# Expert tiles: GpSimd's two result scatters without the wait for TensorE's step signal

## The reference

```python
x = x + attention(layernorm(x), w_lhs, w_rhs)       # softmax((x*w_lhs)(x*w_rhs)^T) x
h = layernorm(x)
logits = h @ router_w.T                              # 4096 x 8, softmax, top 2, gates normalised
hid = gelu_tanh(h @ w_fc[e] + b_fc[e])               # 128 -> 512
y = hid @ w_proj[e] + b_proj[e]                      # 512 -> 128
x = x + sum over the row's two experts of gate * y
```

## Time and profile before

| | us |
|---|---|
| median of 3 runs | 387.25 (387.25 to 387.86) |
| the profiled execution | 387.9 |
| its span, first to last instruction | 386.0 |
| mean granted TensorE clock | 0.914 of full |
| attention | about 0 to 196 |
| expert tiles | about 196 to 366 |
| loading, adding and storing the results | about 366 to 386 |

### The profile page before, as it was taken

How to read it: one execution, slowest core, us unless ns; L and a number is a source line. 1 busy time by engine, 2 the same in 40 slices (tenths; PEclk the granted TensorE clock), 3 DMA queues, 4 the chain that set the end, 5 groups by cost and what they waited for, 6 DMA issues and landing times.

```text
span 386.0 us, 8026 instructions
## 1 busy us (share of the span) xinstructions
PE 312.9 (81%) x2292; PEld 276.0 (72%) x2293; DVE 206.9 (54%) x794; ACT 198.9 (52%) x405; POOL 186.4 (48%) x242
## 2 busy tenths in 40 slices
PE   2689899998799999998778396799999999996000
PEld 1468788876697879886667374699999999996000
DVE  4657488696566677778466433733332333332045
ACT  4216438796037653354538422777776777772000
POOL 7200044092835635376728566555555555557300
PEclk9989998999799998998969798999999999999555
DMA  7910000003100001010321132132222222111099
GB/s 219 440 50 2 1 3 0 3 0 110 36 21 30 28 16 34 23 43 21 94 75 51 41 101 88 56 99 84 78 85 81 77 76 77 42 43 48 28 313 339
DMA packets 17157, 29.48 MB, mean 76 GB/s; under 512 B 3808, under 2 KB 13024, under 8 KB 16864
## 3 DMA queue, kind: packets, MB, share of 16 engines
q1 hardware_dynamic: 12224, 18.46, 14.7%
q0 software_dynamic: 4896, 10.58, 8.3%
HBM read 16.36 MB, written 12.66 MB: 75 GB/s over the span
## 4 chain that ended last, share of the span: by engine, by line
PE 63%; DVE 10%; ACT 7%; another core or an unknown queue 7%; issue 5%; DMA 5%; SPq 1%; DVEq 0%; POOL 0%; ACTq 0%; POOLq 0%
PE av_ps L1211 16%; PE av_ps L1019 14%; PE sc_ps L1194 4%; PE sc_ps L1196 4%; PE sc_ps L1195 4%; PE bank L998 3%; DMA raw_proj<-results 3%; PE bank L999 3%; PE bank L1000 3%; ACT prob L877 2%; PE bank L1182 2%; PE sc_ps L998 2%; PE bank L1011 2%; PE sc_ps L999 2%
## 5 line engine op out<-in xcount | busy, mean ns | idle before, releaser
L835 POOL DMA_INDIRECT results<-prob,result_row x80 | 76.6, 957 | 58.4 <-PE sc_ps L1196 33.0
L749 POOL DMA_INDIRECT slots<-stage,slot x64 | 62.7, 980 | 50.7 <-ACT prob L877 26.7
L1211 PE MATMUL av_ps<-raw_proj,raw_fc 128*128 x640 | 80.3, 280 | 5.3 <-issue 4.3
L1211 PEld LDWEIGHTS av_ps<-raw_proj,raw_fc 128*128 128x128 f32 x640 | 76.5, 196 | 7.4 <-issue 6.8
L955 ACT ACTIVATE raw_fc<-sc_ps,bfc,scale_down 128x256 f32<-128x256 f32 x160 | 77.2, 571 | 2.1 <-PE sc_ps L1196 2.1
L1019 PEld LDWEIGHTS av_ps<-h_all,prob 128*128 128x128 f32 x512 | 70.5, 199 | 8.8 <-issue 4.3
L1019 PE MATMUL av_ps<-h_all,prob 128*128 128x137 f32 x512 | 73.4, 291 | 3.8 <-issue 3.8
L1602 DVE TENSOR_TENSOR h_all<-av_ps,bpr 128x256 f32<-128x256 f32 x40 | 17.0, 425 | 89.7 <-PE sc_ps L1196 60.8
L947 ACT ACTIVATE h_all<-bank 128x512 f16<-128x512 f16 x40 | 23.8, 598 | 58.3 <-PE sc_ps L1196 27.9
L1194 PE MATMUL sc_ps<-h_all,wfc_hi 128*128 128x256 f16 x160 | 44.8, 280 | 3.3 <-issue 2.1
L1195 PE MATMUL sc_ps<-h_all,wfc_hi 128*128 128x256 f16 x160 | 44.7, 280 | 2.7 <-issue 2.7
(11 more groups left out here) (176 smaller groups left out, 528.0 us busy)
## 6 DMA issues: line engine op xcount, KB each, us to landing
slots_in<-slots SPq DMA_DIRECT2D x40, 130.0 KB
raw_fc<-in_w_fc_dram SPq DMA_DIRECT2D x1, 2048.0 KB, 11.0
raw_proj<-in_w_proj_dram SPq DMA_DIRECT2D x1, 2048.0 KB, 15.1
raw_fc<-results SPq DMA_DIRECT2D x2, 1024.0 KB, 6.9
raw_proj<-results SPq DMA_DIRECT2D x2, 1024.0 KB, 11.2
out_dram<-res SPq DMA_DIRECT2D x4, 512.0 KB, 5.0
res<-in_x_dram SPq DMA_DIRECT2D x3, 512.0 KB, 5.5
results<-prob,result_row POOLq DMA_INDIRECT x80
```

What stands on the lines that cost most here:

```text
L749: pool.indirect_dma_start(out=slots[:, :], out_offset=bass.IndirectOffsetOnAxis(ap=slot[:, n, k:k + 1], axis=0), in_=stage[:, b % 2, t, k, ...
L835: pool.indirect_dma_start(out=results[:, :], out_offset=bass.IndirectOffsetOnAxis(ap=result_row[a][:, h:h + 1], axis=0), in_=gated[a][h], ...
L1211: mm = pe.matmul(o, hid[:, a % NH, c, s], wpr[:, e, c, :], start=(c == 0 and h == 0), stop=(c == HC - 1), skip_group_check=True)
```

## The change

The wait on `stepped` goes. GpSimd's step k now waits only for `row_made` and `gated_made` of tile k-4, inside `give_back`.

```diff
                 for i in LAST_SCATTERS.get(k, ()):
                     dispatch(B - 1, i)
                 if k >= 4:
-
-                    if tile_there(k):
-                        pool.wait_ge(stepped, up_at(k))
                     give_back(k - 4, (k - 4) % NR)
```

## The result

The changed kernel takes 404.74 us (median of 4 runs, 403.59 to 406.33) against 387.56 us for the kernel before, measured with it: ratio 1.0433, 95% interval 1.0378 to 1.0488. It is slower by 17 us, where 2 us less were forecast and 390.2 was the top of the range.

The account below looks back on a forecast made before the run. Expert stage taken as TensorE-bound in its plain part, elsewhere held by long runs of GpSimd's indirect DMAs. Terms 0 + 0 - 2.1 + 0.1 = -2.0 us took the profiled 387.9 to 385.9, as median 385.3 us; range 382.9 to 390.2.

Parts of the forecast that it names:

- Step 1: All 36 waits removed (k = 4 to 39): the issue saved is hidden behind TensorE's tile of 3.32 us, 0.
- Step 2: Expert stage's TensorE-bound stretch: two scatters per tile merely start later in the period; 0, bounds -1 to +3 us.
- Step 3: Last tiles: a run of six scatters replaces eight, so the last signal comes sooner; 2.1 us gained, bounds 0.9 and 4.4.
- Step 4: Start of the expert stage: dispatches and scatters fuse into longer runs, only rests move; +0.1 us taken from three pricings.
- the first two: Early part's pricings: by mean progress of TensorE, a gain of 1.8 us; if rests count as before, 0.
- The third, by runs: Early part's pricing with two issues free per run and 1.2 us for each beyond: 2.4 or 4.8 us slower.
- Rival B: Early part: fused runs cost 2.4 to 4.8 us, less 2.1 at the tail; 387.6 to 390, at worst 392; chance 0.32.
- Rival C: TensorE's late signals have their own cause and GpSimd merely waits in step; nothing changes, 387.2 us; chance 0.15.

Follow-up runs that it names:

- the fours: Kernel before, wait kept, but in steps 8 to 35 GpSimd waits every other step, then sends two tiles' four scatters: 399.51 us, ratio 1.0313 on a holding chip.
- the paced tail: Kernel before plus one wait: in step 41 GpSimd awaits TensorE's very last down step before sending tile 37's rows: 385.58 us, ratio 0.9935 on a holding chip.

## Why the prediction was wrong

- **What bounds the kernel now.** Right in its main reading, that long runs of indirect DMAs hold TensorE or its signals; the fours and the paced tail showed it by moving GpSimd's issues and nothing else. Wrong in its last words, "runs of two do not": they hold as well, for 1.4 to 1.5 us an issue, and the kernel before keeps clear of it by only 0.1 to 0.2 us. Its own trace has such signals, at 248.75 and 251.99.
- **Step 1, the wait itself, 0.** Not measured apart; where nothing is held, the whole change gives a ratio of 0.9972 (0.9941 to 1.0003), so the 36 waits are worth at most some 2 us of issuing.
- **Step 2, the plain part. This is the step that failed**: "the same two per tile, the same rest, another phase ... Price 0", with 3 us as the upper bound. It measured 15.2 us when changed alone and 14.3 in the whole. The phase was the price. I forecast the start of a pair well (2 us behind the signal) and saw that the next signal then falls into it, but took one punctual signal, 1.5 us into a run, as proof. That is just where the first issue's 1.43 us is over. The rows had the other evidence: dividing 7.2 and 11.4 us by 5 and 8 gives 1.44 and 1.43.
- What I missed behind it is the feedback. A held signal makes two gates come together, two gates make a run of four, and a run of four holds the next signal. My bound of 0.1 us a tile presupposed that disturbances die out.
- **Step 3, the tail, -2.1.** The size came out (-2.3 in the whole), the way did not: there is no run of six, still one of eight (from 367.21). The last signal came inside it, 8.5 us (six times 1.43) behind its first issue, where it came 11.4 us behind before; why it waited for fewer issues is open, so the size came out by luck. Alone, the edit gains nothing; its first step sends four in a row, which hold a signal by 2.7 us.
- **Step 4, the early part, +0.1 between -1.8 and +4.8.** Measured +3.8 in the trace (4.2 from the first up step's signal on) and 4.3 alone. The bounds held, the value was wrong, and it did not lie "between the first two" prices, which are -1.8 and 0. The third, by runs (2.4 or 4.8 us, the latter for {15,10}), had the right shape: the trace has fifteen issues and then ten.
- **The sum** -2.0 was measured as +17.2. **Rival B**, slower by fused runs, was the right kind and sign (chance 0.31 for slower), but it put the fused runs into the early part alone, gave the plain part 3 us at most for signals held "a little", and stopped at 392 (its own terms add up to 393).
- **Rival C and the skill.** The rows show signals held behind GpSimd's runs on two chips or more, and none held on three others. The Trainium skill, "SBUF — State Buffer", section "SBUF: two separate sides", has TensorE wait for nobody on the engine side. By that rule the change is worth 0, as measured where nothing is held; where it is, the measurement decides. The rule speaks of ports of SBUF, and no run here shows that the holding happens there.

**Open.** What TensorE's signals pass, which issues a signal waits for, what the 1.43 us goes by, whether GpSimd's other work does the same, and what makes a chip hold them. The chips differ, but they were also measured at different times, and other work may have run near them; nothing here separates these.

## What to carry to other kernels

A wait that nobody's data needs can be a pacer. Before removing one, look at what will start when it is gone, where in the bottleneck's period that falls, and whether a delay it causes feeds back into its own length; a bound of "a little per tile" holds only without such a loop. Where late signals of one engine end at fixed multiples behind another's run of issues, divide before pricing: the quotient is how long an issue holds them. And compare on more than one chip before calling a pacing good or bad: this one is worth 17 us on some and nothing on others.

## What the runs showed of the hardware

- The same kernel takes 387.5 us on some chips and 356 us on others, each steady within about 1%. Held signals go with the difference: on the faster kind no signal of TensorE's matmuls comes over 0.1 us behind the matmul's recorded end, even in the changed kernel's run of 63 issues; on the slower kind they are held from the first run of dispatches in the attention on (five issues from 95.87, signal at 103.01). Against the paced tail on the faster kind, the same program up to step 40, the kernel before is 10.8 us later at the first up step's signal (200.24 against 189.40), 26.3 at the ninth's (245.51 against 219.22), 25.8 at the last one's (348.28 against 322.45) and 28.9 at the end (386.0 against 357.1). So a third of it arises in the attention, half in the early part, none in the plain part.
- On the slower kind each indirect DMA of 128 rows delays a TensorE signal that meets it: it arrives 1.4 to 1.5 us per issue behind the run's first, though GpSimd's own part is 0.96 us, every 1.26 us. The last one held by runs of 2, 4, 5, 8, 10 and 15 waited for all of the run's issues; others came after fewer, at six of ten (213.98) or six of eight (375.75, changed kernel).
- While this goes on, TensorE's recorded matmuls can run ahead of their signals: the tail's passes are recorded to 353.56 and the last signal comes at 359.95, DVE starting at 360.24. What other engines see tells more than the matmuls' recorded ends.
